# The maxima of the first two attention slots spread over four projected batches instead of three, and the first two quads loaded earlier

## The chip, the cores and the metric

The kernel runs on one core of a Trainium2 chip. The metric is the device time of one execution in microseconds; the times before are those of three runs, and a profile was taken of one further execution.

## What is computed

A post-norm transformer layer on x of shape (8, 1024, 256), float32:

```python
def ref(x):                                  # 8 batches of 1024 rows, D = 256
    x = layernorm(x + attention(x))          # 16 heads of 16, causal softmax
    return layernorm(x + feed(x))

def attention(x, W_qkv, W_out):
    qkv = einsum('bsd,ndh->bnsh', x, W_qkv); q, k, v = split(qkv, 3)
    attn = softmax(einsum('bnqh,bnkh->bnqk', q, k) / 4 + causal_mask)
    out = einsum('bnqk,bnkh->bnqh', attn, v).reshape(B, -1, S)
    return einsum('bds,nhd->bsd', out, W_out)

def feed(x):     # a mix of neighbouring rows, 9 paths D -> 64 -> D, one chosen per row by an argmax
    ...          # then layernorm(x + chosen) * gamma + beta
```

## The kernel before

The program has three blocks one after the other: `project_stage`, `attend_stage`, `feed_stage`. Each of the five engines has its own list of instructions in each block; they meet through semaphores only, and a block begins when all engines have ended the one before.

**Projection.** Each of the 8 batches is done in two chunks of 512 rows; (b, c) is chunk c of batch b. For each chunk TensorE makes two groups of four transposes of x for the chunk that follows (L511), four products (m = 0 to 3, L545) that give q and k of all heads, and two halves of the values (L555). ScalarE and VectorE split each product into three bfloat16 parts (L436, L397, L440), GpSimd makes the third (L359), and SP's queue stores the parts (`store`, L293) and the values (L297) in the chip's main memory, in order: each of the four stores waits for GpSimd's part, the store of the values for ScalarE. GpSimd's part for m = 3 of a chunk is made early in the next chunk, so `store(b, c)` ends there.

**Maxima.** Attention runs over 32 slots, one for each batch and quad (four heads); it needs the row maxima of each slot's scores beforehand. A slot's maxima are cut into 22 *units* (`UNITS`: heads and a tile of 128 query rows, so a unit is from 128 to 1024 columns wide, some are two heads of 512 or 384). TensorE computes a unit's scores into the one buffer `ps_m` (`Maxima.rows`, L150), VectorE takes the maximum (`Maxima.take`, L176 or L171), and the next unit may start on TensorE only then (L520). Third of each slot's units is the one at which TensorE first transposes the maxima gathered (`Maxima.turn`, L183).

The maxima of slots 0 and 1 are computed within the projection. `ahead(b, c, s)` maps step s of chunk (b, c) to a unit: from batch `AHEAD` = 5 on, all `STEPS_IN` = 8 steps of each chunk, 44 units one after the other, so (5,0) has slot 0's units 0 to 7, (6,0) slot 0's 16 to 21 at steps 0 to 5 and slot 1's first two at steps 6 and 7, and the last chunk (7,1) has four. On TensorE a chunk with units runs: transposes, step 0, product 0, step 1, product 1, step 2, transposes, step 3, values, step 4, product 2, step 5, values, step 6, product 3, step 7. The last chunk has no transposes. On VectorE the takes stand between the four subtractions (L397): steps 0 and 1, m = 0, step 2, m = 1, steps 3 to 5, m = 2, steps 6 and 7, m = 3.

**Loads of the quads.** A slot's first unit waits for 13 loads of its quad (`loaded[0]` at L517, `loaded[1]` at L522): twelve of 128 KB (L86) and `s_vq` of 448 KB (L80), the last. SP issues them in pieces; `PLAN` says behind which chunk's stores which piece goes, as (quad, first load, end). So quad 0's last piece follows the stores of (3,1) and is used first in (5,0); quad 1's follows (5,1) and is used at step 6 of (6,0). Quad 2's last piece goes ahead of the stores of (7,1), and attention's first unit waits for it (L1056).

**Sums of `W_out`.** At the start of chunk (`AHEAD` - 1, 0) TensorE makes a small product (L593) in `ps_m`, ScalarE copies it, GpSimd masks it (`cut`), VectorE reduces it. Batch 0 is written out, batches 1 to `AHEAD` - 2 run in a loop, the rest is written out.

Of the kernel before, what the change touches and what calls it, by code (L numbers as in the profile page):

```python
# [17 lines left out]
CHUNKS = SEQ // CHUNK  # L18
# [31 lines left out]
NU = len(UNITS)  # L50
RBANKS = 2
LOADS = 16 * (2 * len(TERMS) + 1)
AHEAD = 5
STEPS_IN = 8


def identity(eng, tile, done):
# [12 lines left out]
def v_quads(v_rows, b):  # L70

    return v_rows[b].rearrange("t p v -> (t p v)").rearrange("(j p x) -> j p x", j=QUADS, p=P)


def load_piece(sp, quads, qk_parts, v_rows, b, j, first, end):

    qs, ks, vq, loaded = quads
    for d in range(first, end):
        if d == 2 * len(TERMS):
            sp.dma_start(vblocks(vq)[:, j, :, :].rearrange("p t v -> p (t v)"), v_quads(v_rows, b)[j])\  # L80
                .then_inc(loaded[j], 16)
            return
        i = d // 2
        dst, r, part = ((qs, 0, TERMS[i][0]), (ks, HEADS * HD, TERMS[i][1]))[d % 2]
        r += j * QUAD * HD
        sp.dma_start(dst[i:TROWS:len(TERMS), j, :, :],  # L86
                     qk_parts[b, r:r + QUAD * HD, part, :].rearrange("(n h) s -> h n s", h=HD))\
            .then_inc(loaded[j], 16)
# [120 lines left out]
def project_stage(nc, x, w_qkv, qk_parts, v_rows, residual, maxima, weights, stored, head, inputs,  # L209
# [4 lines left out]
    with ExitStack() as ctx:  # L214
# [35 lines left out]

        def ahead(b, c, s):

            k = (CHUNKS * (b - AHEAD) + c) * STEPS_IN + s if isinstance(b, int) else -1
            return divmod(k, NU) if 0 <= k < 2 * NU else None

        w_loaded = sem("p_w_loaded")
# [29 lines left out]
        with nc.Block() as block:  # L286
            @block.sync
            def _(sp):
                def store(b, c):
                    u = b * CHUNKS + c  # L290
                    for m in range(QKM):
                        sp.wait_ge(lo_done, u * QKM + m + 1)
                        sp.dma_start(qk_parts[b, m * P:(m + 1) * P, :, c * CHUNK:(c + 1) * CHUNK],  # L293
                                     parts[:, c, m, :, :]).then_inc(parts_stored[c], 16)
                    sp.wait_ge(v_kept, 2 * u + 2)
                    half = CT * QUAD * VW
                    sp.dma_start(v_quads(v_rows, b)[:, :, c * half:(c + 1) * half].rearrange("j p x -> p j x"),  # L297
                                 v_sb[c][:, :, :, :].rearrange("p j t v -> p j (t v)"))\
                        .then_inc(v_stored[c], 16)

                PLAN = {(2, 0): (0, 0, 3), (2, 1): (0, 3, 6), (3, 0): (0, 6, 9), (3, 1): (0, 9, 13),
                        (4, 0): (1, 0, 3), (4, 1): (1, 3, 6), (5, 0): (1, 6, 9), (5, 1): (1, 9, 13),
                        (6, 1): (2, 0, 4), (7, 0): (2, 4, 8), (7, 1): (2, 8, 13)}

                def turn(b, last):
                    for c in range(CHUNKS):
                        if (b, c) == (BATCH - 1, CHUNKS - 1):
                            load_piece(sp, quads, qk_parts, v_rows, 0, *PLAN[b, c])
                        store(b, c)
                        if (b, c) in PLAN and (b, c) != (BATCH - 1, CHUNKS - 1):  # L310
                            load_piece(sp, quads, qk_parts, v_rows, 0, *PLAN[b, c])
                        if (b, c) == (6, 1):
                            maxima.send(sp, 0, 0)

                for c in range(KC):
                    sp.dma_start(w[:, c, :, :], w_qkv[:, c * P:(c + 1) * P, :].rearrange("n p e -> p n e"))\
                        .then_inc(w_loaded, 16)
                load_weights(sp)
                turn(0, False)
                turn(1, False)  # L320
                for c in range(CHUNKS):

                    sp.wait_ge(parts_stored[c], 16 * QKM)
                    sp.wait_ge(v_stored[c], 16)
                for b in range(2, BATCH):
                    turn(b, b == BATCH - 1)

            @block.gpsimd
            def _(pool):
# [11 lines left out]
                def cut():  # L341
                    runs = P // HEADS
                    pool.wait_ge(wsum_kept, 1)
                    pool.affine_select(out=wide, in_=wide, compare_op=ALU.is_ge, fill=0.0,
                                       base=0, pattern=[[-runs, HEADS], [0, HD]], channel_multiplier=1)\
                        .then_inc(wsum_cut, 1)
                    pool.wait_ge(wsum_cut, 1)
                    pool.affine_select(out=wide, in_=wide, compare_op=ALU.is_ge, fill=0.0,
                                       base=runs - 1, pattern=[[runs, HEADS], [0, HD]], channel_multiplier=-1)\
                        .then_inc(wsum_cut, 1)  # L350

                def turn(b):
                    for c in range(CHUNKS):
                        u = b * CHUNKS + c

                        pool.wait_ge(parts_stored[c], 16 * QKM * b)
                        for m in range(QKM):
                            pool.wait_ge(mid_done, u * QKM + m + 1)
                            pool.tensor_tensor(parts[:, c, m, 2, :], rest[:, m, :], parts[:, c, m, 1, :],  # L359
                                               ALU.subtract).then_inc(lo_done, 1)  # L360

                turn(0)
                with pool.Fori(1, AHEAD - 1) as b:
                    turn(b)
                cut()
                for b in range(AHEAD - 1, BATCH):
                    turn(b)

            @block.vector
            def _(dve):  # L370
# [11 lines left out]
                def turn(b):  # L382
                    for c in range(CHUNKS):
                        u = b * CHUNKS + c

                        def unit(s):
                            if ahead(b, c, s):
                                v, i = ahead(b, c, s)
                                maxima.take(dve, ps_m[:, :, :], shown, v, v, i)
                                if v and i == TURN:  # L390
                                    maxima.split(dve, ps_x, 0)

                        def remain(m):
                            if not isinstance(u, int) or u:
                                dve.wait_ge(lo_done, (u - 1) * QKM + m + 1)
                            dve.wait_ge(hi_done, u * QKM + m + 1)
                            dve.tensor_tensor(rest[:, m, :], ps_qk[:, m, :], parts[:, c, m, 0, :],  # L397
                                              ALU.subtract).then_inc(rest_done, 1)

                        if isinstance(b, int) and (b, c) == (AHEAD, 0):  # L400
                            dve.wait_ge(wsum_done, 1)
                            dve.wait_ge(maxima.causal_made, 2)
                        unit(0)
                        unit(1)
                        remain(0)
                        unit(2)
                        remain(1)
                        unit(3)
                        unit(4)
                        unit(5)  # L410
                        remain(2)
                        unit(6)
                        unit(7)
                        remain(3)
                        if isinstance(b, int) and (b, c) == (AHEAD - 1, 0):
                            dve.wait_ge(wsum_cut, 2)
                            dve.tensor_reduce(residual.wsum[:, :], wide.rearrange("p n i -> p i n"), AX_X, ALU.add)\
                               .then_inc(wsum_done, 1)

                turn(0)  # L420
                with dve.Fori(1, AHEAD - 1) as b:
                    turn(b)
# [80 lines left out]
            def _(pe):  # L503
# [25 lines left out]
                def turn(b, end):  # L529
                    for c in range(CHUNKS):  # L530
# [3 lines left out]
                        def unit(s):  # L534
                            if ahead(b, c, s):
                                rows(*ahead(b, c, s))
# [1229 lines left out]
```

## Time and profile before

| | us |
|---|---|
| median of three runs | 1441.96 (1439.29 to 1444.13) |
| the profiled execution | 1445.97 |
| its span, first to last instruction | 1444.3 |
| TensorE busy in the span | 1378.4 (95%) |
| VectorE busy | 1090.4 (75%) |
| ScalarE busy | 971.8 (67%) |
| mean granted TensorE clock | 0.989 |

Rows of the trace name engines PE (TensorE matmul), PEld (its weight loads), DVE (VectorE), ACT (ScalarE), POOL (GpSimd), SP; a name with a q is the engine's queue. In rows in order of time the first number is the start in us from the span's start, the second the length of the merged run of instructions, "xN" their count, and the bracket the engine's idle time just before and what ended it. Matmul ends are modelled. A group by line has busy time, mean length in ns, and idle time before with its releasers.

### The profile page before, as it was taken

The page shows a single profiled execution, that of the slowest core. Times are in us where ns is not written, and L with a number is a line of the kernel's source. Part 1 is how long each engine was busy: PE and PEld are TensorE (multiplying, and loading weights), DVE is VectorE, ACT ScalarE, POOL GpSimd, SP SyncE. Part 2 cuts the span into 40 slices and gives each one's busy share as a digit, 9 for nine tenths or more (in the row PEclk, how much of TensorE's full clock was granted, in tenths as well). Part 3 has the DMA queues.
Part 4 walks back from the last instruction along what each step waited for, and adds up shares of the span by engine and source line. Part 5 has one row for each costly group of instructions (what it writes and reads, how often), then busy time and mean ns, then how long its engine had stood idle before and what let it go on. Part 6 is the DMA issues. An engine that isn't in the chain of part 4 may idle for free. (4 is left out here: it accounts for less than half of the span.)

```text
span 1444.3 us, 25144 instructions
## 1 busy us (share of the span) xinstructions
PE 1378.4 (95%) x8234; PEld 671.0 (46%) x8282; DVE 1090.4 (75%) x2647; ACT 971.8 (67%) x2121; POOL 428.2 (30%) x561
## 2 busy tenths in 40 slices
PE   7999889999999999999999999999889999999994
PEld 4665443343434343343344343333235666656653
DVE  4224667888888888888888888888335888878875
ACT  4665437887888888878778788888755554545632
POOL 3443222111133133133133133142232542212312
PEclk9999999999999999999999999999999999999997
DMA  8898754322753943843844943944525421110001
GB/s 228 262 296 287 227 179 153 110 87 69 187 98 89 198 95 100 188 95 111 185 97 119 173 104 107 180 111 111 84 73 98 80 74 59 59 44 29 16 29 44
DMA packets 166752, 178.20 MB, mean 123 GB/s; under 512 B 26397, under 2 KB 135784, under 8 KB 166632
## 3 DMA queue, kind: packets, MB, share of 16 engines
q1 hardware_dynamic: 158184, 168.31, 46.0%
q10 hardware_dynamic: 8448, 8.39, 1.8%
q8 instruction: 63, 1.03, 0.3%
q14 instruction: 57, 0.47, 0.1%
HBM read 109.79 MB, written 66.06 MB: 122 GB/s over the span
## 5 line engine op out<-in xcount | busy, mean ns | idle before, releaser
L979 ACT ACTIVATE a_probs<-a_ps_s 128x512 f32<-128x512 f32 (+3 forms) x1536 | 661.1, 495 | 162.5 <-PE a_ps_s L1084 133.8
L176 DVE CUSTOM_DVE_ANT_0 h_space<-a_ps_m,a_causal 128x768 f32<-128x768 f32 (+4 forms) x624 | 524.1, 887 | 82.3 <-PE a_ps_m L150 78.2
L1084 PE MATMUL a_ps_s<-s_qs,s_ks 99*128 99x512 bf16 (+3 forms) x1536 | 408.7, 328 | 7.6 <-ACT a_probs L979 4.2
L150 PE MATMUL a_ps_m<-s_ks,s_qs 96*128 96x512 bf16 (+3 forms) x1440 | 343.1, 325 | 5.0 <-DVE a_mx L176 2.9
L929 POOL TENSOR_SCALAR_AFFINE_SELECT a_probs<-a_probs 128x512 f32<-128x512 f32 x256 | 163.9, 640 | 606.9 <-ACT a_probs L979 605.5
L1041 PE MATMUL a_ps_o<-a_probs,s_vq 128*32 128x512 f32 (+3 forms) x3072 | 302.7, 496 | 1.3 <-ACT a_o_sb L958 1.2
L1084 PEld LDWEIGHTS a_ps_s<-s_qs,s_ks 99*128 99x128 bf16 x1536 | 137.3, 96 | 343.4 <-ACT a_probs L979 242.0
L150 PEld LDWEIGHTS a_ps_m<-s_ks,s_qs 96*128 96x128 bf16 x1440 | 131.1, 98 | 61.6 <-DVE a_mx L176 6.6
L1555 PE MATMUL f_ps_o<-f_w,f_hm 128*128 128x256 f32 (+1 forms) x640 | 151.5, 385 | 0.9 <-DVE f_y L1462 0.9
L1555 PEld LDWEIGHTS f_ps_o<-f_w,f_hm 128*128 128x128 f32 (+1 forms) x640 | 121.4, 192 | 27.6 <-issue 8.4
L1041 PEld LDWEIGHTS a_ps_o<-a_probs,s_vq 128*32 128x32 f32 x3072 | 72.6, 109 | 109.5 <-issue 93.7
L545 PE MATMUL p_ps_qk<-p_x_t,p_wqk 128*128 128x512 f32 x256 | 120.0, 598 | 0.1
L359 POOL TENSOR_TENSOR h_space<-p_rest,h_space 128x512 bf16<-128x512 f32 x64 | 73.6, 1156 | 141.8 <-ACT h_space L440 141.7
L397 DVE TENSOR_TENSOR p_rest<-p_ps_qk,h_space 128x512 f32<-128x512 f32 x64 | 44.1, 690 | 87.8 <-ACT h_space L436 78.5
L1263 POOL TENSOR_TENSOR f_rs_b<-f_ve_b,f_half 128x4 f32<-128x4 f32 x32 | 35.0, 1094 | 227.4 <-DVE f_ve_b L1418 227.3
L176 DVE CUSTOM_DVE_ANT_0 a_aw_sb<-a_ps_m,a_causal 128x768 f32<-128x768 f32 (+4 forms) x96 | 80.6, 887 | 17.4 <-PE a_ps_m L150 16.8
L436 ACT ACTIVATE h_space<-p_ps_qk 128x512 bf16<-128x512 f32 x64 | 38.2, 597 | 62.6 <-PE p_ps_qk L545 62.5
L1361 ACT ACTIVATE f_hid<-f_ps_h,f_bias 128x512 f32<-128x512 f32 x64 | 44.0, 687 | 52.5 <-PE f_ps_h L1576 51.6
L1576 PE MATMUL f_ps_h<-h_space,f_w 128*128 128x512 f32 x160 | 76.8, 625 | 0.0
L1366 ACT ACTIVATE f_hid<-f_ps_h,f_bias 64x512 f32<-64x512 f32 x16 | 10.9, 682 | 94.3 <-PE f_ps_h L1576 94.3
L1576 PE MATMUL f_ps_h<-f_xm,f_w 128*128 128x512 f32 x160 | 72.3, 595 | 0.0
L545 PEld LDWEIGHTS p_ps_qk<-p_x_t,p_wqk 128*128 128x128 f32 x256 | 47.4, 192 | 40.2 <-issue 34.8
(138 smaller groups left out, 1315.5 us busy)
## 6 DMA issues: line engine op xcount, KB each, us to landing
qk_parts<-h_space SPq DMA_DIRECT2D x64, 384.0 KB, 4.0
s_qs<-qk_parts SPq DMA_DIRECT2D x192, 128.0 KB, 2.8
s_ks<-qk_parts SPq DMA_DIRECT2D x192, 128.0 KB, 2.8
s_vq<-v_rows SPq DMA_DIRECT2D x32, 448.0 KB, 4.8
f_x_in<-in_L_attn_x_dram ACTq DMA_DIRECT2D x16, 512.0 KB, 6.7
heads_out<-a_o_sb SPq DMA_DIRECT2D x128, 64.0 KB
f_x_in<-in_L_attn_x_dram SPq DMA_DIRECT2D x8, 1024.0 KB, 8.8
f_a_in<-heads_out SPq DMA_DIRECT2D x64, 128.0 KB, 9.1
```

The source lines that it names most:

```text
L150: last = pe.matmul(out, self.qs[0:TROWS, j, h, q], self.ks[0:TROWS, j, h, s:s + wide], start=k == 0, stop=mask is None)
L176: taken = dve.tensor_tensor_reduce(out=shown[:, i % 2, k * CHUNK:k * CHUNK + width], in0=row, in1=self.causal[:, SEQ - width:SEQ], scale=1 ...
L359: pool.tensor_tensor(parts[:, c, m, 2, :], rest[:, m, :], parts[:, c, m, 1, :], ALU.subtract).then_inc(lo_done, 1)
L397: dve.tensor_tensor(rest[:, m, :], ps_qk[:, m, :], parts[:, c, m, 0, :], ALU.subtract).then_inc(rest_done, 1)
L545: last = pe.matmul(ps_qk[:, m, :], wqk[:, k, m, :], x_t[:, c, k, :], start=(k == 0), stop=(k == KC - 1))
L929: pool.affine_select(out=tile, in_=tile, compare_op=ALU.is_ge, fill=0.0, base=0, pattern=[[0, QUAD], [1, P]], channel_multiplier=-1)\
L979: act.activation(probs[:, st % PB, h, 0:width], ps_s[:, n % BANKS, 0:width], ACT.Exp, scale=SCALE).then_inc(exps[h % 2], 1)
L1041: last = pe.matmul(ps_o[h * OW:(h + 1) * OW, off:CHUNK], vblocks(vq)[:, j, kt, VBLOCK[h] * HD:(VBLOCK[h] + 2) * HD], probs[:, st % PB, h, ...
L1084: pe.matmul(ps_s[:, n % BANKS, 0:width], ks[0:MROWS, j, h, kt * P:(kt + 1) * P], qs[0:MROWS, j, h, q0:q0 + width], start=True, stop=True)\
L1361: act.activation(hid[:, m, :], ps_h[:, (m + 1) % 2, :], ACT.Identity, bias=bias[:, m:m + 1]).then_inc(h_kept, 1)
L1555: ins = pe.matmul(ps_o[:, t // 2, t % 2, :], hm[0:rows, c, m, t * P:(t + 1) * P], w2_sb[0:rows, m, :], start=(m == 0), stop=(m == LAST))
L1576: ins = pe.matmul(ps_h[:, i % 2, :], w1_sb[:, k, 2 * m:2 * m + 2, :].rearrange("d p m -> d (p m)"), xm[e][:, k, c * CHUNK:(c + 1) * CHUNK] ...
```

## The change

`AHEAD` goes from 5 to 4 and the steps used from all eight to six: 0, 1, 2, 4, 5, 7. The 44 units then fill the chunks from (4,0) to (7,0) with six each, and the last chunk (7,1) has two, at steps 0 and 1. Slot 1's first unit comes at step 5 of (5,1). The sums of `W_out` move to (3,0), and the loop runs over batches 1 and 2. `PLAN` issues quad 0 in three pieces behind (2,0), (2,1), (3,0) and quad 1 in four behind (3,1), (4,0), (4,1), (5,0); quad 2 stays.

```diff
-AHEAD = 5
-STEPS_IN = 8
+AHEAD = 4
+STEPS_IN = (0, 1, 2, 4, 5, 7)
...
         def ahead(b, c, s):
 
-            k = (CHUNKS * (b - AHEAD) + c) * STEPS_IN + s if isinstance(b, int) else -1
+            if not isinstance(b, int) or s not in STEPS_IN:
+                return None
+            k = (CHUNKS * (b - AHEAD) + c) * len(STEPS_IN) + STEPS_IN.index(s)
             return divmod(k, NU) if 0 <= k < 2 * NU else None
...
-                PLAN = {(2, 0): (0, 0, 3), (2, 1): (0, 3, 6), (3, 0): (0, 6, 9), (3, 1): (0, 9, 13),
-                        (4, 0): (1, 0, 3), (4, 1): (1, 3, 6), (5, 0): (1, 6, 9), (5, 1): (1, 9, 13),
+                PLAN = {(2, 0): (0, 0, 4), (2, 1): (0, 4, 8), (3, 0): (0, 8, 13),
+                        (3, 1): (1, 0, 3), (4, 0): (1, 3, 6), (4, 1): (1, 6, 9), (5, 0): (1, 9, 13),
                         (6, 1): (2, 0, 4), (7, 0): (2, 4, 8), (7, 1): (2, 8, 13)}
```

## Rows read from the trace of the kernel before

**Rows 1.** The page's slices: TensorE's busy tenths in 40 slices of 36.1 us.

```profile
PE   7999889999999999999999999999889999999994
```

**Rows 2.** Windows (stretch, its length, busy us by engine, PEclk, DMA share, GB/s): without and with units.

```profile
90.85:102.05 11.20, 11.20 (x40) 6.99 (x39) 2.77 (x5) 6.80 (x14) 4.59 (x5) 1.00 1.00 305
139.26:155.33 16.07, 14.82 (x62) 8.53 (x61) 10.79 (x19) 7.19 (x15) 4.86 (x5) 1.00 0.68 215
```

**Rows 3.** Groups by line of TensorE: the units within the projection.

```profile
L150 PE MATMUL p_ps_m<-s_ks,s_qs 96*128 96x512 bf16 (+3 forms) x96 | 23.2, 327 | 9.1 <-DVE a_mx L176 7.8 <-DMA s_vq<-v_rows 1.0 <-DVE a_mx L171 0.4
```

**Rows 4.** TensorE in order of time: a plain chunk's start, then waits of units.

```profile
113.25 0.60 PE L511 MATMUL p_ps_t<-s_ident,f_x_in 128*128 128x128 f32 x4
113.69 3.60 PE L545 MATMUL p_ps_qk<-p_x_t,p_wqk 128*128 128x512 f32 x8
...
140.48 0.60 PE L150 MATMUL p_ps_m<-s_ks,s_qs 96*128 96x512 bf16 x2 [0.62 <-DVE a_mx L176]
...
156.90 0.55 PE L150 MATMUL p_ps_m<-s_ks,s_qs 96*128 96x512 bf16 x2 [0.97 <-DVE a_mx L176]
...
174.15 0.28 PE L183 MATMUL p_ps_m<-s_ident,a_mx 128*32 128x128 f32 x1 [0.89 <-DVE a_mx L176]
...
190.51 0.50 PE L150 MATMUL p_ps_m<-s_ks,s_qs 96*128 96x512 bf16 x2 [0.76 <-DVE a_mx L176]
...
195.98 0.55 PE L150 MATMUL p_ps_m<-s_ks,s_qs 96*128 96x512 bf16 x2 [0.49 <-DVE a_mx L176]
...
206.74 0.50 PE L150 MATMUL p_ps_m<-s_ks,s_qs 96*128 96x384 bf16 x2 [1.41 <-DVE a_mx L176]
```

**Rows 5.** TensorE in order of time: chunk (6,0) and its load wait; the stage's end.

```profile
155.33 0.60 PE L511 MATMUL p_ps_t<-s_ident,f_x_in 128*128 128x128 f32 x4
...
170.19 0.48 PE L150 MATMUL p_ps_m<-s_ks,s_qs 96*128 96x512 bf16 x2 [0.96 <-DMA s_vq<-v_rows]
...
219.24 1.99 PE L555 MATMUL p_ps_v<-p_w,p_x_t 128*128 128x256 f32 x8 [0.81 <-ACT f_a_in L445]
222.91 0.48 PE L150 MATMUL a_ps_m<-s_ks,s_qs 96*128 96x512 bf16 x2 [1.68 <-PEq L286]
```

**Rows 6.** SP's queue in order of time: start and issue time of single DMAs.

```profile
93.99 0.62 SPq L297 DMA_DIRECT2D v_rows<-h_space  x1
...
96.84 1.48 SPq L86 DMA_DIRECT2D s_qs<-qk_parts  x1
...
163.98 0.60 SPq L80 DMA_DIRECT2D s_vq<-v_rows  x1
...
216.78 0.58 SPq L80 DMA_DIRECT2D s_vq<-v_rows  x1
```

**Rows 7.** Landing of `s_vq`: four of 60 to 235, then quad 0's, then quad 2's.

```profile
DMA to landing us min/median/max: 3.9/5.1/6.1
...
s_vq<-v_rows SPq DMA_DIRECT2D x1, 448.0 KB, 5.2
...
s_vq<-v_rows SPq DMA_DIRECT2D x1, 448.0 KB, 5.0
```

**Rows 8.** TensorE in order of time in `feed_stage`: waits and the matmuls behind them.

```profile
1154.03 0.39 PE L1613 MATMUL f_ps_h<-f_pick_t,f_widen 128*128 128x512 bf16 x1 [2.47 <-DVE f_hm L1457]
...
1281.37 2.32 PE L1555 MATMUL f_ps_o<-f_w,f_hm 128*128 128x256 f32 x10
1285.26 0.39 PE L1613 MATMUL f_ps_h<-f_pick_t,f_widen 128*128 128x512 bf16 x1 [1.56 <-DVE f_hm L1457]
...
1286.08 4.01 PE L1555 MATMUL f_ps_o<-f_w,f_hm 128*128 128x256 f32 x10
...
1418.19 8.89 PE L1555 MATMUL f_ps_o<-f_w,f_hm 128*128 128x256 f32 x40 [0.88 <-DVE f_y L1462]
```

**Rows 9.** Windows as in rows 2: behind the wait near 1285, and after TensorE's last matmul.

```profile
1286.50:1290.00 3.50, 3.50 (x10) 2.72 (x10) 0.48 (x1) 0.00 (x0) 0.00 (x0) 0.53 0.44 153
1429.00:1430.00 1.00, 0.00 (x0) 0.00 (x0) 0.38 (x2) 0.49 (x1) 0.72 (x1) 0.88 0.00 0
```

## The prediction

> **What bounds the kernel now.** I read the page's slices first, then the windows, the groups by line, the order of time of TensorE, and last the order of time of SP's queue with its landings. The slices show TensorE at 0.9 or more nearly everywhere; the exceptions are the very start, the end, and slices 4 to 6, which are the stretch from about 124 to 223 us that the change touches [rows 1]. The windows show why. A chunk of the projection without units is 11.20 us long and TensorE is busy in all of it; a chunk with eight units is 16.07 us long with TensorE busy 14.82 [rows 2]. So the plain chunks have no room: a unit moved into one lengthens it by its whole length. Only the waits between units can be won.
>
> By line, the units of this stage wait 9.1 us, of which 7.8 and 0.4 end with a maximum that VectorE takes and 1.0 with a load; the transpose of the maxima adds 0.89 [rows 3, 4]. In the order of time these waits stand in two places of a chunk, at step 0 and at step 3, both just behind four transposes. A unit can't start until the maximum of the unit before it is taken (they share one buffer), and four transposes take only 0.44 us from start to next start (113.25 to 113.69), while their row is modelled 0.60 long; a wait is therefore its row's idle plus 0.16 [rows 4]. The wait follows the width of the unit before: 0.65 after 640 columns, 0.78 after 768, 0.92 after 896, 1.05 after 1024, 1.13 after twice 512 (idle 0.49, 0.62, 0.76, 0.89, 0.97) [rows 4].
>
> **The change part by part.** *The units themselves.* 44 units before and after, the same matmuls on TensorE and the same maxima on VectorE; nothing is gained or lost in their busy time.
>
> *Step 3 goes.* Its six waits are what is left of 7.8 + 0.4 + 0.89 = 9.09 after the five of step 0 (0.62, 0.97, 0.89, 0.76, 1.41, together 4.65): 4.44, with 6 x 0.16 it is 5.40 us [rows 3, 4]. The unit after step 2 now stands at step 4, behind transposes and half of the values. A step of products or values is (11.20 - 2 x 0.44) / 6 = 1.72 us, more than any wait above, so nothing takes its place. **-5.4.** Step 6 goes too, and with it the load wait there, 0.96 + 0.17 = **-1.13** [rows 5].
>
> *Step 0 stays and comes seven times* (the first, in chunk (4,0), waits for a load instead). Before: 4.65 + 5 x 0.16 = 5.45. After, by the unit at step 7 of the chunk ahead: 640, 768, twice 512, 1024, 768, 896 columns, then 640 into the last chunk, which has no transposes to cover 0.44: 0.65 + 0.78 + 1.13 + 1.05 + 0.78 + 0.92 + 1.09 = 6.40. **+0.95.**
>
> *The loads.* This is the part that decides. Each piece is issued behind the stores of its chunk, and these wait for GpSimd's last part, which comes some 4 us into the next chunk. Quad 0's last piece now follows the stores of (3,0); its first unit is at step 0 of (4,0). The `v_rows` store of (3,0) is issued at 93.99 [rows 6]; the sums of `W_out`, 0.86 us of TensorE, move from (4,0) to (3,0) and so shift it to 94.85. Behind it go five loads instead of three. SP needs some 0.65 for the store, 0.7 for the first load and 1.4 to 1.5 for each next one (the third started at 96.84 and took 1.48), so `s_vq` is issued near 100.6. The four such loads of this stretch took 3.9 to 6.1 us to land; the nearest, quad 0's own at the same load on the DMA engines, 5.2 [rows 7]. It lands near 105.8. TensorE asks at 102.05 + 0.44 = 102.49. **+3.4** (2.1 at 3.9, 4.3 at 6.1; the DMA share is already 1.00 at 305 GB/s there [rows 2], so a later landing is likelier than an earlier one).
>
> Quad 1's last piece follows the stores of (5,0), and its first unit moves from step 6 of (6,0) to step 5 of (5,1). Before, the chunk began at 155.33, `s_vq` went out at 163.98, 8.65 later, and TensorE went on at 170.19, 14.86 after the chunk's start, having asked at 13.73 [rows 5, 6]. After, the same piece comes behind the same kind of unit (twice 512 at step 7), so the arrival stays at 14.8. The question is asked sooner: without the unit and wait of step 3 (1.13), the unit of step 5 and half of the values (2.05) and with narrower units (0.2), at 10.3. **+4.5** (2.4 at a landing of 3.9). The cover that held before, half a chunk of other work, is gone.
>
> *The end of the stage.* The last chunk starts at 206.74 - 1.57 = 205.17 [rows 4], and TensorE ends 15.79 later (219.24 + 1.72) [rows 5]. It now has two units instead of four (0.6 less), no wait at step 3 (1.5 less) and a shorter one at step 0 (0.5 less): 13.2. Attention begins 1.95 behind that, as now (222.91) [rows 5], so at 15.2. But attention's first unit needs quad 2, whose `s_vq` is issued 11.6 us into that chunk (216.78) and lands 5.0 later [rows 6, 7]; with 0.4 sooner by the narrower unit ahead it is there at 16.2 and used at 16.3. **+1.1** (0 to 2.2).
>
> *Edits at nothing.* GpSimd's two masks, the copy and the reduction of the sums move a batch forward; GpSimd is busy 4.59 of 11.20 and VectorE 2.77 there [rows 2], cover enough. Batch 3 leaves the loop, and the plain chunks are 11.20 inside the loop as outside. The stores behind the five loads are issued some 2 us later; the buffers they free are wanted a chunk later. With six units VectorE has 6 x 1.1 + 4 x 0.69, some 9.4 of 14 us.
>
> Sum so far: -5.4 - 1.13 + 0.95 + 3.4 + 4.5 + 1.1 = **+3.4 us**.
>
> *The clock.* The two load waits, 3.4 and 4.5, are longer than any wait of TensorE in the rows after its start. Near 1285 a wait of 1.56 ended with the granted clock at half: ten matmuls took 4.01 us where the same ten took 2.32, and the stretch had 0.53; a wait of 2.47 left it full [rows 8, 9]. At the end TensorE stops at 1427.08 and the clock falls near 1429.8, 2.7 us later [rows 8, 9]. Both new waits are longer than that. If some 3.3 us at half follow each time (the stretch of [rows 9]), 0.7 and 1.8 of it pass in the wait itself and 2.6 and 1.5 do half of their work: 1.3 + 0.75. **+2.1** (0 if it holds, 2 x 1.69 = 3.4 as near 1285). The Trainium skill has this rule, in TensorE: Matmul & The Clock Gate, section HAM oscillation: a kernel that waits for DMA between bursts restarts cold each time and pays half of the throttled time. It speaks against this change; the row near 1285 agrees with it, the row with 2.47 shows that not each wait does it.
>
> Total +5.5. Against the profiled execution (1445.97, of which the span is 1444.3) that is 1451.5; the median of the three runs is 4.0 lower, and so the forecast is 1441.96 + 5.5 = **1447.5**.
>
> **The rivals.** *The same waits, the clock held:* +3.4, 1445.4. For it: 2.47 without a fall. Against: both waits outlast the 2.7.
> *The loads land quickly,* all three as the quickest row, 3.9: -5.58 + 2.1 + 2.4 + 0 = -1.1, 1440.9. Against it: the quickest of four, and the DMA share of 1.00. The Trainium skill, DMA: Bandwidth & Descriptors, section Anatomy of one DMA, gives a DMA some 2 us beside its bytes; at the row's 305 GB/s a load of 448 KB would be an estimated 3.5 us, and the sum -1.9. The rows, at 5.1 in the middle, speak against.
> *The loads are there when asked* (the other side, faster): only the -5.58 is left, 1436.4. It decides where `s_vq` of both quads lands within some 1.8 us of its issue; or where I am wrong on which store the piece waits for. No row of such a load is near it.
> *The queue backs up:* the pieces now are 4, 4, 5 and the stores behind them late, on engines already full. Landing 1.5 later than 6.1 for both quads gives 5.8 + 6.0, with 2.2 at the end and 3.4 for the clock: +11.8, 1453.8. Waits that reappear at step 4 would end near there too.
>
> **How the numbers follow.** Forecast 0.52, clock held 0.22, quick landing 0.10, there when asked 0.05, backed up 0.11. About 0.3%, 4.3 us, is what a measurement of this kernel can tell from no change; slower than 1446.3 are most of the forecast (0.47), the backed-up case and a little of the held clock: 0.63. Within: 0.32. Faster: 0.05. The range leaves out the two lowest cases and the top of the highest: 1443 to 1453; the likeliest case alone is 1445.4 to 1450.
>
> **What would show it.** Right: no idle behind the second transposes of a chunk, seven waits of 0.5 to 1.0 at step 0; one wait on `s_vq` of 3 to 4 us near 102.5 and one of 4 to 5 in chunk (5,1); attention beginning with a wait on quad 2; half clock behind one or both. Wrong: no DMA wait at either place, which would make the kernel faster, or step 4 waiting for VectorE.

## The result and the profile after

The changed kernel is slower. The medians are 1451.52 us (1450.79 to 1456.08, seven runs) against 1444.13 us for the kernel before, run beside it (1439.29 to 1446.83, seven runs); the ratio is 1.0069, with a 95% interval of 1.0053 to 1.0085. Two repetitions below gave 1.0071 and 1.0074. So the change costs some 10 us (0.0069 x 1444.13 = 10.0; by the interval 7.7 to 12.3), and the forecast was 5.5. The two medians alone lie 7.4 us apart, and the seven runs before spread over 7.5 us, so the amount is known only to some 2 us. The direction and most of the places were right; the amount was not.

The profiled execution took 1453.64 us, its span is 1451.6, 7.3 more than that of before. In `after`, lines of the code stand two further down than in the rows of before (L513 is the transposes, L547 the products, L557 the values, L295 and L299 the stores).

The page's slices of the changed kernel, to be held against [rows 1]:

```profile
PE   7999898999999999999999999999889999999995
```

The weak slices near the units are still there. The windows of the changed kernel (columns as in [rows 2]) show a plain chunk, and then chunk (5,0) with six units:

```profile
91.10:102.31 11.21, 11.21 (x42) 6.86 (x41) 3.27 (x5) 6.87 (x14) 4.60 (x5) 1.00 1.01 318
134.81:149.42 14.61, 13.99 (x58) 8.27 (x57) 8.87 (x17) 7.17 (x15) 4.73 (x5) 1.00 0.75 237
```

The chunk with units now waits 14.61 - 13.99 = 0.62 us, half of the 1.25 of [rows 2], so within a chunk the change does what it says. The group by line of the units in the projection answers [rows 3]:

```profile
L150 PE MATMUL p_ps_m<-s_ks,s_qs 96*128 96x512 bf16 (+3 forms) x96 | 23.8, 334 | 12.1 <-DMA s_vq<-v_rows 7.8 <-DVE a_mx L176 4.4
```

The waits on VectorE have shrunk from 7.8 + 0.4 to 4.4, and waits on a load have grown from 1.0 to 7.8. Their places stand in TensorE's order of time (columns as in [rows 4, 5]):

```profile
102.31 0.60 PE L513 MATMUL p_ps_t<-s_ident,f_x_in 128*128 128x128 f32 x4
106.29 0.82 PE L150 MATMUL p_ps_m<-s_ks,s_qs 96*128 96x512 bf16 x2 [3.39 <-DMA s_vq<-v_rows]
106.90 3.06 PE L547 MATMUL p_ps_qk<-p_x_t,p_wqk 128*128 128x512 f32 x4
109.80 0.60 PE L150 MATMUL p_ps_m<-s_ks,s_qs 96*128 96x512 bf16 x2
...
121.90 0.45 PE L150 MATMUL p_ps_m<-s_ks,s_qs 96*128 96x512 bf16 x2 [0.48 <-DVE a_mx L176]
...
158.02 1.88 PE L547 MATMUL p_ps_qk<-p_x_t,p_wqk 128*128 128x512 f32 x4
164.28 0.80 PE L150 MATMUL p_ps_m<-s_ks,s_qs 96*128 96x512 bf16 x2 [4.38 <-DMA s_vq<-v_rows]
164.87 3.09 PE L557 MATMUL p_ps_v<-p_w,p_x_t 128*128 128x256 f32 x8
167.80 1.88 PE L547 MATMUL p_ps_qk<-p_x_t,p_wqk 128*128 128x512 f32 x4
...
214.48 0.60 PE L150 MATMUL p_ps_m<-s_ks,s_qs 96*128 96x512 bf16 x2 [0.93 <-DVE a_mx L176]
...
224.82 1.99 PE L557 MATMUL p_ps_v<-p_w,p_x_t 128*128 128x256 f32 x8 [0.81 <-ACT f_a_in L447]
230.24 0.48 PE L150 MATMUL a_ps_m<-s_ks,s_qs 96*128 96x512 bf16 x2 [3.43 <-PEq L288]
234.12 0.59 PE L150 MATMUL a_ps_m<-s_ks,s_qs 96*128 96x512 bf16 x2 [0.36 <-DVE a_mrest L193]
```

Read three things here. First, the two load waits, 3.39 and 4.38 us, at step 0 of (4,0) and step 5 of (5,1). Second, what runs behind each: four products take 3.06 where the same four took 1.88, eight values 3.09, so TensorE is at its lower clock. The windows of these two places say it outright (the granted clock is the third number from the end, 1.00 being 2.4 GHz and 0.50 being 1.2 GHz):

```profile
106.60:109.80 3.20, 3.20 (x6) 1.32 (x5) 0.96 (x2) 0.00 (x0) 0.00 (x0) 0.58 1.08 389
164.90:167.80 2.90, 2.90 (x10) 2.37 (x9) 1.57 (x3) 0.00 (x0) 0.00 (x0) 0.59 0.20 68
```

Third, attention's first unit, at 230.24, stands behind 3.43 us of idle, where it was 1.68 [rows 5], and what ended that is the start of the block (PEq), not a load. The queue of SP shows why (start, issue time):

```profile
100.67 0.58 SPq L80 DMA_DIRECT2D s_vq<-v_rows  x1
...
158.09 0.59 SPq L80 DMA_DIRECT2D s_vq<-v_rows  x1
...
218.17 0.71 SPq L86 DMA_DIRECT2D s_qs<-qk_parts  x1
...
224.52 0.58 SPq L80 DMA_DIRECT2D s_vq<-v_rows  x1
225.15 3.40 SPq L295 DMA_DIRECT2D qk_parts<-h_space  x4
228.59 1.06 SPq L299 DMA_DIRECT2D v_rows<-f_a_in  x1
```

Nine loads of quad 2, four behind the stores of (7,0) and five ahead of those of (7,1), are issued one after the other from 218.17 to 225.1. Behind them stand the last five stores, four of the parts and one of the values; SP is done at 228.59 + 1.06 = 229.65, and only then can the next block begin. In the kernel before, the same queue is not late: its last row starts at 221.95, when ScalarE has the last values (its row ends at 221.93):

```profile
217.41 4.07 SPq L293 DMA_DIRECT2D qk_parts<-h_space  x4
221.95 0.36 SPq L297 DMA_DIRECT2D v_rows<-f_a_in  x1
```

The DMA view of the three stretches, which answers [rows 7], has the landing of `s_vq` behind its issue in us, for quads 0, 1 and 2:

```profile
s_vq<-v_rows SPq DMA_DIRECT2D x1, 448.0 KB, 5.6
...
s_vq<-v_rows SPq DMA_DIRECT2D x1, 448.0 KB, 6.0
...
s_vq<-v_rows SPq DMA_DIRECT2D x1, 448.0 KB, 4.2
```

Quad 2's is there at 224.52 + 4.2 = 228.7, ahead of the end of SP's stores (229.65).

**Where the 7.3 us of span come from.** From the transposes of (4,0) to attention's first unit, before took 222.91 - 102.05 = 120.86 us and after takes 230.24 - 102.31 = 127.93: +7.07. The start of that stretch is 0.26 later, and from attention's first unit to the end both take 1221.4. By steps: -5.40 for step 3, -1.13 for step 6, +0.95 for step 0, the forecast's values, which the rows bear out; the load waits +3.55 (106.29 - 102.31 - 0.43) and +4.54 (164.28 - 158.02 - 1.72); the stage end +1.75 (from the last values, 226.54, to 230.24 are 3.70, were 1.95); the clock +2.83 (unit and product, 109.80 - 106.29 = 3.51 against 2.14 in an experiment with the full clock at this place, unit and values 3.52 against 2.06). The sum is 7.09.

### The profile page after: what moved, and what is told of

Same layout as the page of the kernel before. It is cut to its first block and busy times, and to the rows that moved or that the text cites. A ratio compares the mean times of both kernels' runs of the same rounds, so it can differ in the third digit from the quotient of the medians.

```text
span 1451.6 us, 25096 instructions
## 1 busy us (share of the span) xinstructions
PE 1381.0 (95%) x8234; PEld 673.2 (46%) x8282; DVE 1090.0 (75%) x2647; ACT 971.9 (67%) x2121; POOL 428.0 (29%) x561
## 5 line engine op out<-in xcount | busy, mean ns | idle before, releaser
L547 PE MATMUL p_ps_qk<-p_x_t,p_wqk 128*128 128x512 f32 x256 | 121.5, 604 | 0.1
L176 DVE CUSTOM_DVE_ANT_0 a_inv_in<-p_ps_m,a_causal 128x768 f32<-128x768 f32 (+5 forms) x48 | 42.1, 891 | 48.4 <-PE p_ps_m L150 48.1
```

The lines of the kernel that those rows point to most:

```text
L176: taken = dve.tensor_tensor_reduce(out=shown[:, i % 2, k * CHUNK:k * CHUNK + width], in0=row, in1=self.causal[:, SEQ - width:SEQ], scale=1 ...
L547: last = pe.matmul(ps_qk[:, m, :], wqk[:, k, m, :], x_t[:, c, k, :], start=(k == 0), stop=(k == KC - 1))
```

## The experiments

The theory after this reading: the spread of the units is worth 5.6 us as forecast, and what it costs is three places in which something is too late: two loads, and SP's last stores; the clock is lost behind the two loads, and may be behind the stores. The first rival is that a stretch with units in four batches is slow by itself; the second is that the changed `PLAN` disturbs the plain chunks.

**The first two quads' loads one chunk earlier still.** All else as in the change.

```diff
-PLAN = {(2, 0): (0, 0, 4), (2, 1): (0, 4, 8), (3, 0): (0, 8, 13),
-        (3, 1): (1, 0, 3), (4, 0): (1, 3, 6), (4, 1): (1, 6, 9), (5, 0): (1, 9, 13),
+PLAN = {(2, 0): (0, 0, 6), (2, 1): (0, 6, 13),
+        (3, 0): (1, 0, 4), (3, 1): (1, 4, 8), (4, 0): (1, 8, 13),
```

> The changed kernel, with the loads of quads 0 and 1 issued earlier still: quad 0 whole behind the stores of (2,0) and (2,1), quad 1 behind (3,0), (3,1) and (4,0). Units and steps are those of the change. Theory (the two load waits of 3.55 and 4.54 us, and the half clock behind them, 2.9 us, are what the change costs): both waits and the half clock go, 11.0 us less than the changed kernel, 3.7 us less than the kernel before (ratio near 0.997). Rival A (the spread itself costs: seven waits at step 0, more chunks out of the loop): stays 5 to 7 us above the kernel before. Rival B (the DMA engines are full there, so that earlier loads only push back stores and loads of x): the waits turn up at other places, 0 to 4 us above the kernel before.

Measured: ratio 0.9998 (0.9989 to 1.0007). The stretch is 102.39 to 219.70, 117.31 us, -3.55 against before. Both load waits are gone, and the units do not wait anywhere that they did not in the forecast. But the ratio shows little of it, where 3.7 us less than before were expected, and the trace of this kernel shows where it went (TensorE, in order of time):

```profile
219.70 0.80 PE L150 MATMUL a_ps_m<-s_ks,s_qs 96*128 96x512 bf16 x2 [3.74 <-PEq L288]
220.30 1.06 PE L1086 MATMUL a_ps_s<-s_qs,s_ks 99*128 99x512 bf16 x2
...
225.50 0.59 PE L150 MATMUL a_ps_m<-s_ks,s_qs 96*128 96x512 bf16 x2 [0.20 <-DVE a_mrest L193]
```

Attention starts behind 3.74 us of idle, and two matmuls that take 0.60 at the full clock take 1.06. From the first of these rows to the last, 225.50 - 219.70 = 5.80 us pass; in the changed kernel's profiled execution it was 234.12 - 230.24 = 3.88, and in before 3.89. So the late stores cost up to twice: 2 us of idle, and 1.9 us of clock behind it.

**Quad 2's loads earlier, none ahead of the last stores.** All else as in the change.

```diff
-(6, 1): (2, 0, 4), (7, 0): (2, 4, 8), (7, 1): (2, 8, 13)}
+(5, 1): (2, 0, 4), (6, 0): (2, 4, 8), (6, 1): (2, 8, 13)}
...
-if (b, c) == (BATCH - 1, CHUNKS - 1):
-    load_piece(sp, quads, qk_parts, v_rows, 0, *PLAN[b, c])
 store(b, c)
-if (b, c) in PLAN and (b, c) != (BATCH - 1, CHUNKS - 1):
+if (b, c) in PLAN:
     load_piece(sp, quads, qk_parts, v_rows, 0, *PLAN[b, c])
```

> The changed kernel, with quad 2's three pieces behind the stores of (5,1), (6,0) and (6,1), so that no load stands ahead of the stores of the last chunk; all else as in the change, the two load waits too. Theory (SP, which issues nine loads and then the last five stores, ends the stage): attention's first unit comes 2 us or less behind TensorE's last value matmul instead of 3.7, so 1.7 us less than the changed kernel, 5.6 above the kernel before. Rival (the prediction's own: attention waits for quad 2's last load): the same 1.7 us go, but SP's last store is issued no earlier. Rival (the barrier between the blocks is what it is): no change.

Measured: ratio 1.0060 (1.0047 to 1.0073). The stretch is 103.32 to 229.69, 126.37 us, +5.51. In the trace (SP, then TensorE) SP's stores stand behind no loads, the last is issued when the values are there, and attention begins as before:

```profile
222.52 5.73 SPq L295 DMA_DIRECT2D qk_parts<-h_space  x4
228.73 0.37 SPq L299 DMA_DIRECT2D v_rows<-f_a_in  x1
...
229.69 0.48 PE L150 MATMUL a_ps_m<-s_ks,s_qs 96*128 96x512 bf16 x2 [1.68 <-PEq L288]
```

The idle ahead of attention is back at 1.68. In all eleven traces of this document attention's first unit starts 0.59 to 0.61 us behind the end of SP's last issue, whether the idle before it is 1.68 or 3.74 us, and in the change quad 2's last load had landed by then. That settles the cause of the longer stage end: SP's queue. In time, 5.6 us above before were expected and the ratio gives 8.7 (6.8 to 10.5); the stretch is as expected, and the table below has what else this execution shows.

**Both together.** The spread of the change, with all loads early and none ahead of the last stores (the two diffs above).

> The changed kernel with its own six steps 0, 1, 2, 4, 5, 7, and quads 0, 1 and 2 all loaded early (the tables of the two runs with early loads together). Theory (the spread gains 5.40 + 1.13 - 0.95 = 5.6 us; the load waits, the half clock and SP's late last stores take it away): 5.6 us less than the kernel before, ratio 0.996, attention's first unit 1.9 us behind TensorE's last value matmul, no half clock before 900 us. Rival (the run with quads 0 and 1 early was no faster than the kernel before because the spread gains nothing in the times): ratio 1.000.

Measured: ratio 0.9975 (0.9961 to 0.9990). The stretch is 102.43 to 217.70, 115.27 us, -5.59 against before, where the first three steps of the forecast add up to -5.58:

```profile
217.70 0.48 PE L150 MATMUL a_ps_m<-s_ks,s_qs 96*128 96x512 bf16 x2 [1.69 <-PEq L288]
```

So the first rival falls: the spread itself gains what was worked out, and the change loses it to the loads and stores that come too late, and to the clock behind them.

**The clock kept up in the load waits.** The change with 8 and 10 extra matmuls (L520; the rows count each as two) ahead of the two load waits. Their result is used by nobody; ps_m is overwritten by the unit.

```diff
+def fill(n):
+    for _ in range(n):
+        pe.matmul(ps_m[:, 0, 0:D], ones, wout[:, 0, :], start=True, stop=True)
...
+    pe.wait_ge(wsum_kept, 1)
+    fill(8)
     pe.wait_ge(loaded[0], LOADS)
-    pe.wait_ge(wsum_kept, 1)
...
+    fill(10)
     pe.wait_ge(loaded[1], LOADS)
```

> The changed kernel, with eight extra matmuls of 128x256 into the free buffer of the units ahead of the wait for quad 0 and ten ahead of that for quad 1 (0.43 us each, 3.4 and 4.3 us in all); their results are overwritten and used by nobody. TensorE is then busy while the loads come. Theory (the matmuls behind the waits ran at half clock because TensorE stood still): the granted clock stays full, the product behind the first wait takes 1.9 us instead of 3.1 and the values behind the second 1.9 instead of 3.1, 2.9 us less than the changed kernel, 4.4 above the kernel before. Rival (they ran slowly for another reason, such as the load's own traffic): as the changed kernel, 7.3 above. If the extra matmuls outlast the loads, up to 0.3 us more at each place.

Measured: ratio 1.0058 (1.0045 to 1.0071). TensorE in order of time:

```profile
102.91 3.62 PE L520 MATMUL p_ps_m<-f_wout,a_aw_sb 128*128 128x256 f32 x16
106.44 0.50 PE L150 MATMUL p_ps_m<-s_ks,s_qs 96*128 96x512 bf16 x2
106.78 1.88 PE L553 MATMUL p_ps_qk<-p_x_t,p_wqk 128*128 128x512 f32 x4
...
158.51 4.48 PE L520 MATMUL p_ps_m<-f_wout,a_aw_sb 128*128 128x256 f32 x20
163.59 0.50 PE L150 MATMUL p_ps_m<-s_ks,s_qs 96*128 96x512 bf16 x2 [0.59 <-DMA s_vq<-v_rows]
163.92 1.89 PE L563 MATMUL p_ps_v<-p_w,p_x_t 128*128 128x256 f32 x8
```

The loads come as late as before, but the products behind take 1.88 and the values 1.89. The stretch is 125.73 us, 2.2 shorter than in the change. That 2.9 were expected is put down by the rows to the second wait, 163.59 - 158.51 = 5.08 where it was 4.54, and not to the matmuls behind it. So the lost clock is real, and by the rows worth some 2.8 us beside the waits themselves; the times alone do not show it, as the intervals of this ratio and of the change's overlap. In time, 4.4 us above before were expected and the ratio gives 8.4 (6.5 to 10.2); the table below gives 6.6 for this trace. At attention's start, behind 3.54 us of idle, the clock fell here, as it had not in the profiled execution of the change.

**Only the bare waits left.** The same extra matmuls, and quad 2's loads early.

> The change with quad 2's pieces earlier (behind (5,1), (6,0), (6,1), so that SP's last stores stand behind no loads) and with 8 and 10 extra matmuls of 128x256 in front of the two load waits, whose result nobody uses. Only the bare waits on s_vq of quads 0 and 1 are left of what made the change slower. Theory: the stretch from (4,0)'s transposes to attention's first unit is +5.5 (quad 2 earlier, as seen) - 2.2 (clock kept, as seen) = +3.3 against before, some 124.1 us, attention starts after 1.7 us of idle at the full clock, no half clock near 102 to 236 us, and with 0.3 us outside the span the time is 1.0025 of before. Rival: something beside the waits, the clock and SP's last stores costs the changed kernel some 2 us that its trace doesn't show; then the stretch is the same and the time 1.004 or more.

**The change again, beside it.**

> The change as it is, beside the kernel with the bare waits. Theory: 1.007 as measured twice, with attention's start behind 3.4 to 3.7 us of idle and the clock falling there in some executions; the difference to the bare waits is the clock of the two waits (2.9), SP's last stores (1.8) and in some executions the clock at attention's start (up to 1.9): 4.7 to 6.6 us, 0.0033 to 0.0046 of the time. Rival: the same difference is under 0.0025.

Measured: 1.0031 (1.0018 to 1.0045) for the bare waits, 1.0074 (1.0055 to 1.0093) for the change, run on one chip. The stretch with the bare waits is 103.26 to 227.32, 124.06 us as expected, attention starts behind 1.69 us of idle, and the granted clock of the stretch is 1.00. The expected 1.0025 lies in the interval, but so does the rival's 1.004: the times do not exclude a further 2 us that no row shows. The intervals of the two kernels lie apart. The difference of the ratios, 0.0043 or 6.2 us, lies where the clock of the waits (2.8), the late stores (1.8) and the clock at attention's start (1.9) add up to 6.5. The trace of the change has this last part in it:

```profile
230.81 0.80 PE L150 MATMUL a_ps_m<-s_ks,s_qs 96*128 96x512 bf16 x2 [3.66 <-PEq L288]
231.41 1.06 PE L1086 MATMUL a_ps_s<-s_qs,s_ks 99*128 99x512 bf16 x2
...
236.61 0.59 PE L150 MATMUL a_ps_m<-s_ks,s_qs 96*128 96x512 bf16 x2 [0.30 <-DVE a_mrest L193]
```

**The change once more, on the chip of the next kernel.**

> The changed kernel as it is, once more, beside the runs that differ from it. Theory: 7 us more than the kernel before (ratio 1.005), waits of 3.5 and 4.5 us for quads 0 and 1 and half clock behind each, attention's first unit 3.7 us behind the last value matmul. Rival (the first comparison, ratio 1.0069, holds and some 3 us come from outside the stretch of the change): 1.007, with the rest of the program, from attention's first unit on, longer than 1221 us.

Measured: 1.0071 (1.0056 to 1.0086). Attention starts behind 3.72 us of idle with the clock at half, 5.79 us from its first unit to the row that in the fence above starts at 236.61.

**The change's `PLAN` in the kernel before.** Units as before, loads as in the change.

```diff
-PLAN = {(2, 0): (0, 0, 3), (2, 1): (0, 3, 6), (3, 0): (0, 6, 9), (3, 1): (0, 9, 13),
-        (4, 0): (1, 0, 3), (4, 1): (1, 3, 6), (5, 0): (1, 6, 9), (5, 1): (1, 9, 13),
+PLAN = {(2, 0): (0, 0, 4), (2, 1): (0, 4, 8), (3, 0): (0, 8, 13),
+        (3, 1): (1, 0, 3), (4, 0): (1, 3, 6), (4, 1): (1, 6, 9), (5, 0): (1, 9, 13),
```

> The kernel before with the change's table of loads alone: units, steps and batches as before, quad 0 behind (2,0), (2,1), (3,0) and quad 1 behind (3,1) to (5,0). Theory (earlier loads are only worth the wait that they end): the load wait at step 6 of (6,0) goes, 1.13 us, and nothing else moves: 1.1 us less than the kernel before, ratio 0.999, no difference that can be measured in the times, but to be seen in the order of time. Rival (full DMA engines): new waits for stores or for x, slower by 1 us or more.

Measured: 0.9999 (0.9986 to 1.0011), where 0.999 was expected. The second rival falls: earlier loads alone neither cost nor gain what can be measured. The load wait of (6,0) is gone from the trace, but of its 1.13 us the stretch keeps only 0.49, as attention starts later behind the last values:

```profile
224.20 0.52 PE L150 MATMUL a_ps_m<-s_ks,s_qs 96*128 96x512 bf16 x2 [2.32 <-PEq L286]
```

On SP's queue one load of quad 2 took 1.23 us to issue where it took 0.59 in before, and the last store ended 0.65 later behind the last values. So one slow issue is enough there: the kernel before has next to nothing to spare at this place; whether the earlier loads have to do with that one issue is not shown.

**No unit behind a transpose.** Step 0 is given up for step 6, so that a product or half of the values stands ahead of each unit; all loads early, none ahead of the last stores.

```diff
-STEPS_IN = (0, 1, 2, 4, 5, 7)
+STEPS_IN = (1, 2, 4, 5, 6, 7)
```

> The changed kernel with steps 1, 2, 4, 5, 6, 7 instead of 0, 1, 2, 4, 5, 7, so that no two units are next to each other with only transposes between, and all of quads 0 to 2 loaded early as in the two runs before. Theory: all waits of units go, at step 0 (5.45 us before, 6.4 in the changed kernel) and at step 3 (5.40), and the load wait (1.13): 12.0 us less than the kernel before, ratio near 0.992. Rival (VectorE, with two units between its last two subtractions, falls behind and TensorE waits at steps 6 and 7 or at the products): 4 to 8 us of it are lost. Rival B (full DMA engines): waits for x or for stores in batches 2 to 4.

Measured: 1431.84 us, ratio 0.9925 (0.9912 to 0.9938), faster than both kernels. The group by line of its units has no idle time left:

```profile
L150 PE MATMUL p_ps_m<-s_ks,s_qs 96*128 96x512 bf16 (+3 forms) x96 | 23.1, 326 | 0.0
```

In its page's slices of TensorE the weak ones of this stage are back at 0.9:

```profile
PE   7999999999999999999999999999889999999994
```

The stretch is 102.14 to 210.96, 108.82 us, -12.04 against before: the 5.59 of the kernel with all loads early, and the seven waits of step 0, 6.40, that it still had.

**Does the trace account for the ratios?** For each profiled execution, against the one of before: how much later (4,0)'s transposes start, the stretch, the time from attention's first unit to the row that starts at 226.80 in before and 234.12 in the change (3.89 in before), and what lies outside the span (1.67 in before). The last column is the ratio less 1, times the median of before beside it, with its interval.

| kernel | start | stretch | attention's start | outside | sum, us | by the ratio, us |
|---|---|---|---|---|---|---|
| the change | 0.26 | 7.07 | 0.0 | 0.4 | 7.7 | 10.0 (7.7 to 12.3) |
| the change again | 0.54 | 7.49 | 1.9 | 0.4 | 10.3 | 10.2 (8.1 to 12.4) |
| the change, beside the bare waits | 0.52 | 7.38 | 1.9 | 0.3 | 10.1 | 10.7 (7.9 to 13.4) |
| bare waits | 1.21 | 3.20 | 0.0 | 0.4 | 4.8 | 4.5 (2.6 to 6.5) |
| clock kept in the waits | 0.42 | 4.87 | 1.0 | 0.3 | 6.6 | 8.4 (6.5 to 10.2) |
| quad 2 earlier | 1.27 | 5.51 | 0.0 | 0.3 | 7.1 | 8.7 (6.8 to 10.5) |
| first quads earlier | 0.34 | -3.55 | 1.9 | 0.3 | -1.0 | -0.3 (-1.6 to 1.0) |
| all loads early | 0.38 | -5.59 | 0.0 | 0.4 | -4.8 | -3.6 (-5.6 to -1.4) |
| no unit behind a transpose | 0.09 | -12.04 | 0.0 | 0.4 | -11.6 | -10.8 (-12.7 to -8.9) |
| `PLAN` alone | 1.78 | -0.49 | 1.5 | 0.1 | 2.9 | -0.1 (-2.0 to 1.6) |

Nine of ten sums lie within the interval, or at its edge. The tenth is one execution of the kernel that is nearly before, with a start 1.78 later and a clock that fell at attention's start; whether most of its executions have these is not shown. The start and the 0.3 to 0.4 outside the span are not traced to a cause here, and neither is part of what the change does by design.

The sums leave out the rest of the program, behind that row, and compare one execution with the times of several. The rest took 1217.5 us in before and in the change, 1212.3 and 1212.1 in the two repetitions of the change, and 1211.8 to 1216.6 in the others. The clock makes most of this: from 1020 to 1100 us, in `feed_stage`, the mean granted clock is 0.91 in before and in the change, 1.00 and 0.98 in the repetitions. So the spans of two profiled executions can differ by 5 us for reasons that are not in the edit, and the table shows the stage only.

## Why the prediction was right and wrong

Two steps failed: the end of the stage, where the prediction had attention wait for a load and it waited for SP's stores, and the clock, which was put too low behind the two load waits and at nothing at attention's start.

**What bounds the kernel, the units, step 3, step 6, step 0:** right, to 0.01 us as the kernel with all loads early shows (-5.59 against -5.58), and with nothing taking their place. The wait at step 0 follows the width of the unit before, as worked out from [rows 4].

**The loads:** right, 3.55 and 4.54 us where 3.4 and 4.5 were forecast. The second came out as counted from SP's rows: `s_vq` was issued 158.09 - 149.42 = 8.67 us into its chunk (8.65 forecast) and landed 6.0 behind that, where the arrival of before, 6.1 behind the issue, had been carried over. In the first, misses cancelled: the store ahead went out at 95.18 and not 94.85, two loads and not three took some 1.5, and `s_vq` was still issued at 100.67 (100.6 forecast); it landed 5.6 us later, 5.2 had been taken, and TensorE asked 0.25 later. That the sum is so near is partly luck. The rivals *quick landing* and *there when asked* needed 3.9 and 1.8, and the estimate of 3.5 us beside them lies under all three landings of the change too (5.6, 6.0, 4.2).

**The end of the stage:** the step that failed in its mechanism. The last chunk took 13.15 us (13.2 forecast), and quad 2's `s_vq` went out 11.1 us into it (11.2 forecast) and was there 1.5 us before attention's first unit. So attention did not wait for it. What I left out is that a block ends when all engines have ended, and SP's last five stores stand behind those same loads: the shorter chunk took away the time in which SP had issued them. +1.75 where +1.1 was forecast, in the other two traces of the change 2.0, and it is the quad 2 experiment, with the fixed 0.6 us behind SP's last issue, that shows it. I had asked of the moved DMAs when they land, and not what stands behind them on the queue.

**The clock:** the term that was mis-sized. It fell behind both load waits, as forecast, but cost 2.83 and not 2.1 (3.05 and 3.25 in the other two traces of the change): by the two windows of it the half clock lasts to some 109.3 (106.6 + 2 x 0.42 x 3.2) and 167.3 (164.9 + 2 x 0.41 x 2.9), so 3.0 us lie behind the end of each wait and do half of their work, where I had put 2.6 and 1.5 there, the rest into the wait. And the third long wait, at attention's start, had no clock in the sum: I had it at the 1.95 of before plus 1.1. In two of the three traces of the change, behind 3.66 and 3.72 us, the clock fell there too and cost another 1.9; in the third, behind 3.43, it held. The Trainium skill has it so in TensorE: Matmul & The Clock Gate, section HAM oscillation, that a kernel which waits between bursts restarts at the lower clock each time. Both load waits agree in all three traces of the change; attention's start, where 3.43 held, does not. The rival *clock held* fell.

**From the span to the time:** the forecast added its sum to the median as it stood, but in the change 0.3 to 0.4 us more lie outside the span, and the start is 0.3 to 0.5 later; no run shows why. With those, with the clock (0.7 + 1.9), the stage end (0.7 to 0.9) and the loads (0.2), the forecast 5.5 becomes 9.6 to 10.1 (5.5 + 0.3 + 0.3 + 2.6 + 0.7 + 0.2 = 9.6), and 7.7 in an execution in which the clock holds at attention's start; the ratios gave 10.0 to 10.7.

**The rival *queue backs up*:** its time, 1453.8, is nearer than the forecast to what the ratio gives from the median before, 1441.96 x 1.0069 = 1451.9, but its mechanism did not show: it needed `s_vq` of both quads at 7.6 us, and they took 5.6 and 6.0. The queue was late only at SP's end.

## What to carry to other kernels

When a chunk is made shorter, count what each queue still has to issue in it, up to the end of the block: a load that lands in time can still hold up the stores behind it, and the block with them. A load that moves closer to its use can cost its wait and then the clock behind it, as here, so a gain in the waits of one engine is worth having only once the loads have been issued early enough; here the same spread is 1.0069 with late loads, 0.9975 with early ones, and 0.9925 with the units moved away from the transposes as well. Waits of one buffer go where another step's work already covers them: here that was a matter of which six steps are used.

## What the runs showed of the hardware

The clock at attention's start is seen behind eleven waits, one in each trace: behind 1.68 or 1.69 us of idle it held in each of five (before, quad 2 earlier, no unit behind a transpose, all loads early, bare waits); behind 2.32, 3.54, 3.66, 3.72 and 3.74 it fell; behind 3.43 it held. So the same program can lose 1.9 us there in one execution and not in another, and the profiled execution of the change happened to be one that did not. What decides it is not shown; the length of the idle alone does not, as 2.32 fell and 3.43 held.

The time of a whole execution goes with its mean granted clock: those of before at 0.994 have spans of 1437.8 to 1439.3 us, those at 0.989 1444.1 to 1444.4. The profiled execution behind the forecast, at 0.989 and 1444.3, was one of the longest. It held the clock at attention's start, and lost it in `feed_stage`, where the mean from 1020 to 1100 us is 0.91.

Matmuls that nobody needs kept the clock at 2.4 GHz through both load waits. In the first they cost nothing: the unit began 3.97 us after the chunk's transposes (106.44 - 102.47), and 3.98 in the change (106.29 - 102.31). In the second they did not fill all of it, 0.59 to 0.83 us of idle stayed, and the clock held there too.
